# Queries and keys of an fp32 projection taken in two crosswise half-contractions on TensorE's two row groups, behind the last two score units of a turn

## The reference

```python
xn = layernorm(x)                                   # no scale, no shift
q, k, v = xn @ wq[h] + bq, xn @ wk[h] + bk, xn @ wv[h] + bv        # 16 heads of 8 columns
att = softmax(q k^T / sqrt(8)) v                    # per head, 256 x 256
a = concat(att) @ wo.T + bo
xr, xk = mu_r*xn + (1-mu_r)*prev(xn), mu_k*xn + (1-mu_k)*prev(xn)  # prev: one token back
f = sigmoid(xr @ W_r) * (square(relu(xk @ W_k)) @ W_v)
out = x + a + f
```

## Time and profile before

| | |
|---|---|
| median of 3 runs | 490.2 us (489.94 to 491.75) |
| the profiled execution's own time | 489.46 us |
| its span in the trace | 487.1 us |
| mean granted TensorE clock over the span | 0.971 |
| busy: TensorE, VectorE, ScalarE, GpSimd | 461.3, 422.2, 385.6, 339.6 us |

### The profile page before, as it was taken

How to read it: one execution, slowest core, us unless ns; L and a number is a source line. 1 busy time by engine, 2 the same in 40 slices (tenths; PEclk the granted TensorE clock), 3 DMA queues, 4 the chain that set the end, 5 groups by cost and what they waited for, 6 DMA issues and landing times.

```text
span 487.1 us, 15612 instructions
## 1 busy us (share of the span) xinstructions
PE 461.3 (95%) x5238; PEld 263.7 (54%) x5238; DVE 422.2 (87%) x886; ACT 385.6 (79%) x834; POOL 339.6 (70%) x611
## 2 busy tenths in 40 slices
PE   5599999999999999999999999999999999999994
PEld 4145555555555555555555555555655555555452
DVE  7578999999989999899998999999998999988831
ACT  2038888888878888888888888888888888888883
POOL 6567778777777877777777777777787777766220
PEclk9559999999999999999999999999999999999998
DMA  4443355444344544344455454344444443445100
GB/s 140 131 119 95 118 154 150 127 137 140 109 124 142 152 129 144 117 118 125 131 153 143 129 145 123 102 133 142 152 147 126 132 124 109 134 137 143 46 15 22
DMA packets 85837, 60.43 MB, mean 124 GB/s; under 512 B 6192, under 2 KB 73392, under 8 KB 85808
## 3 DMA queue, kind: packets, MB, share of 16 engines
q1 hardware_dynamic: 85808, 60.06, 42.2%
HBM read 29.89 MB, written 29.36 MB: 122 GB/s over the span
## 4 chain that ended last, share of the span: by engine, by line
PE 86%; DVE 6%; issue 4%; ACT 2%; DMA 1%; DVEq 0%; ACTq 0%; SPq 0%; POOL 0%; POOLq 0%
PE bank_exp L613 24%; PE bank_val L565 24%; PE bank_max L623 5%; PE misc_b L689 4%; PE misc_a L640 4%; PE misc_a L659 4%; DVE neg_max L496 4%; PE misc_c L585 3%; PE misc_a L697 3%; PE misc_b L650 3%; PE misc_a L708 2%; PE misc_b L589 2%; PE misc_c L573 1%; PE misc_c L667 1%; PE misc_b L672 1%
## 5 line engine op out<-in xcount | busy, mean ns | idle before, releaser
L496 DVE TENSOR_REDUCE neg_max<-bank_max 128x2 f32<-128x512 f32 x512 | 329.4, 686 | 35.2 <-PE bank_max L623 30.4
L406 ACT ACTIVATE probs<-bank_exp 128x512 f32<-128x512 f32 x512 | 279.0, 597 | 46.1 <-PE bank_exp L613 43.6
L613 PE MATMUL bank_exp<-ops 51*128 51x256 bf16 x1024 | 169.9, 271 | 7.5 <-DVE neg_max L496 2.4
L623 PE MATMUL bank_max<-ops 48*128 48x256 bf16 x1024 | 176.8, 279 | 0.0
L565 PE MATMUL bank_val<-probs,val 128*25 128x256 f32 x2048 | 138.4, 383 | 1.2 <-ACT probs L406 1.2
L613 PEld LDWEIGHTS bank_exp<-ops 51*128 51x128 bf16 x1024 | 65.5, 94 | 109.2 <-issue 88.2
L565 PEld LDWEIGHTS bank_val<-probs,val 128*25 128x25 f32 x2048 | 56.5, 103 | 41.1 <-issue 20.2
L623 PEld LDWEIGHTS bank_max<-ops 48*128 48x128 bf16 x1024 | 61.9, 95 | 1.2
L365 POOL TENSOR_TENSOR rstd<-var_eps,minus_half 128x2 f32<-128x2 f32 x32 | 22.9, 714 | 38.2 <-DVE var_eps L528 38.2
L321 POOL TENSOR_SCALAR xn<-x_in,moments,rstd 128x128 f32<-128x128 f32 x62 | 49.3, 801 | 0.0
L360 POOL TENSOR_TENSOR mixed_x<-mixed_x,xn_t 128x512 f32<-128x512 f32 x32 | 40.6, 1269 | 2.5
(11 more groups left out here) (67 smaller groups left out, 612.5 us busy)
## 6 DMA issues: line engine op xcount, KB each, us to landing
ops<-spill SPq DMA_DIRECT2D x128, 192.0 KB, 3.3
spill<-qk_h SPq DMA_DIRECT2D x64, 192.0 KB, 3.3
spill<-qk_m SPq DMA_DIRECT2D x64, 128.0 KB, 1.9
x_in<-x SPq DMA_DIRECT2D x32, 128.0 KB, 2.2
spill<-qk_l SPq DMA_DIRECT2D x32, 128.0 KB, 1.8
y_out<-y SPq DMA_DIRECT2D x32, 128.0 KB, 1.9
ops<-shift SPq DMA_DIRECT2D x128, 6.0 KB
w<-weights SPq DMA_DIRECT2D x1, 448.0 KB, 2.9
```

What stands on the lines that cost most here:

```text
L406: nc.scalar.activation(probs[g % 2][:, u % G, :, :], bank_exp[u % 2][:, :, :], ACT.Exp, scale=SCALE).then_inc(exp_done[u], 1)
L496: nc.vector.tensor_reduce(out=neg_max[hf][:, :, r, pr], in_=bank_max[v % 2][:, :, :], axis=AX_X, op=ALU.max, negate=True).then_inc(max_don ...
L613: exp_mm = nc.tensor.matmul(bank_exp[r][:, i, :], ops[p][rows, hf, 1, pr, i * P:(i + 1) * P], ops[p][rows, hf, 0, pr, :], start=True, stop ...
L623: max_mm = nc.tensor.matmul(bank_max[r][:, i, :], of[rows, max_hf, 0, max_pr, i * P:(i + 1) * P], of[rows, max_hf, 1, max_pr, :], start=Tr ...
```

## The change

The two full projections become four half-contractions. `project` is replaced by `project_half`, called twice. Without `swap` (behind unit 14) it multiplies the queries' lower 64 channels in the lower row group into `misc_c` and the keys' upper 64 channels in the upper row group into `misc_b`, both with start and without stop. With `swap` (behind unit 15) it multiplies the other halves, crosswise, and adds them to the same banks. The first step has all the waits that `project` had. The second waits for both halves of the first, on two new semaphores. The hidden layer still stands behind it at u = 15.

```diff
+        qk_half = [sem(f"{a}_half") for a in "qk"]
...
-            def project(c, n, live):
-                moving = xn_t[(c + 3) % TURN][:, 1:1 + S]
-                pe.wait_ge(xn_t_done, n(3))
-                after(pe, shift_done[0], n(1))
-                after(pe, qk_rest_done[0], n(2))
-                if not live(2):
-                    pe.wait_ge(weights_in, 16 * N_WEIGHT_DMAS)
-                nc.tensor.matmul(misc_c[:, 0:S], w[:, W_Q, :], moving, start=True,
-                                 stop=True).then_inc(qk_psum[0], 1)
-                after(pe, val_done, n(1))
-                after(pe, qk_rest_done[1], n(2))
-                nc.tensor.matmul(misc_b[:, 0:S], w[:, W_K, :], moving, start=True,
-                                 stop=True).then_inc(qk_psum[1], 1)
+            def project_half(c, n, live, swap):
+
+                moving = xn_t[(c + 3) % TURN]
+                lower, upper = slice(0, RG), slice(RG, P)
+                if not swap:
+                    pe.wait_ge(xn_t_done, n(3))
+                    after(pe, shift_done[0], n(1))
+                    after(pe, qk_rest_done[0], n(2))
+                    after(pe, val_done, n(1))
+                    after(pe, qk_rest_done[1], n(2))
+                    if not live(2):
+                        pe.wait_ge(weights_in, 16 * N_WEIGHT_DMAS)
+                else:
+
+                    pe.wait_ge(qk_half[0], n(3))
+                    pe.wait_ge(qk_half[1], n(3))
+                q_rows, k_rows = (upper, lower) if swap else (lower, upper)
+                q_mm = nc.tensor.matmul(misc_c[:, 0:S], w[q_rows, W_Q, :], moving[q_rows, 1:1 + S], start=not swap,
+                                        stop=swap)
+                k_mm = nc.tensor.matmul(misc_b[:, 0:S], w[k_rows, W_K, :], moving[k_rows, 1:1 + S], start=not swap,
+                                        stop=swap)
+                for a, mm in enumerate((q_mm, k_mm)):
+                    mm.then_inc(qk_psum[a] if swap else qk_half[a], 1)
...
                     if u == HALF and live(2) and not live(1):
-                        project(c, n, live)
+                        project_half(c, n, live, False)
+                    if u == HALF + 1 and live(2) and not live(1):
+                        project_half(c, n, live, True)
...
-                    if u == 15 and live(3) and (live(1) or not live(2)):
-                        project(c, n, live)
+                    if u >= 14 and live(3) and (live(1) or not live(2)):
+                        project_half(c, n, live, u == 15)
```

## The result

The changed kernel takes 497.78 us (median of 4 runs, 496.38 to 499.3) against 490.07 (4 runs, 488.0 to 491.75): ratio 1.016, 95% interval 1.0109 to 1.0211. On a second chip it took 495.91 against 489.79, ratio 1.0134 (1.0085 to 1.0183). The forecast was 492.4, with 497.5 as the upper end. So 6 to 8 us were lost where about 2 were forecast.

What follows compares the result with a forecast made beforehand. TensorE's own sequence was taken as the bound, VectorE and ScalarE close behind. +0.06 us a turn over 30 turns (+1.8) and +0.3 at the start gave +2.1 to 2.2: 490.2 + 2.2 = 492.4 us, range 487.0 to 497.5.

Steps and rivals of the forecast that it cites:

- the halves run side by side and overtake: In each projection step on TensorE, two halves share 0.43 us, the keys' first starting before the queries' second.
- the exposed first weights: Ahead of the hidden layer on TensorE: a first weight load of 0.11 us, which the queries had before.
- the 0.09: On TensorE before and after the hidden layer: 0.09 us lost at each change between row groups and 128 rows.
- the self-wait: Ahead of step 2, TensorE waits for step 1's completion: a new cost of 0.16 us a turn.
- step 2 starts at about 1.04, 0.16 after unit 15 has ended: Times from unit 14's start: step 1 done at 0.83, weight load at 0.94, weights 0.11, then step 2's stream.
- the bounds given: For the wait ahead of step 2: 0 to 0.30 us, the upper with two waits in series, each 0.07 more.
- the forecast case: The whole kernel at 490.5 to 494.5 us, with a chance of 0.52.
- A saving or a loss in one turn therefore counts about 30 times: Over the hidden layer's turns of 13.97 us: +0.06 us a turn, 30 turns, gives +1.8 us.
- ScalarE's stretch as unbroken: ScalarE shows no idle time from the queries to units 0 and 1's exponentials, so a 0.25 us delay passes on.
- slower through ScalarE: Rival: ScalarE's 0.25 us delay is not absorbed, +0.13 a turn on top, +6.0 in all, 496.2 us; chance 0.18.
- The start: At the first projection, two steps and the wait delay the first operands: +0.3 us once, bounds 0 and 0.75.
- a third of 0.52 with 0.18 and 0.10: Chances for slower: a third of the 490.5 to 494.5 case, ScalarE's delay 0.18, strict matmul order 0.10; stated 0.42.

Runs made afterwards that it cites:

- the two runs with nothing between: Kernel before with the keys' full product waiting for the queries': 501.66 us; changed kernel with both steps behind unit 15: 508.5 us.
- the covered wait: Changed kernel with step 1 moved behind unit 13 ahead of the values' product and step 2 behind unit 14: 504.79 us, ratio 1.0324.
- the start left as before: Changed kernel with the first two projections as two full products each, as in the kernel before: 495.52 us, ratio 1.0141.
- no-wait run: Changed kernel with the second step taking the same halves as the first, so it needs no wait: 492.46 us, ratio 1.005.

## Why the prediction was wrong

**Right.** No time is saved on the stream; the halves run side by side and overtake; step 1 needs no change of mode and its weights are preloaded; unit 15 comes 0.66 after unit 14 (0.67); the hidden layer takes over the exposed first weights; the 0.09 ahead of it and behind it stay. The sign, and that the self-wait is the part that costs.

**The term that was mis-sized: "step 2 starts at about 1.04, 0.16 after unit 15 has ended".** The streams of step 2 start at 1.09 and 1.12, 0.20 and 0.23 after it. The first load comes 0.16 after the modelled end of step 1, not 0.11, and why is open (0.12 in the two runs with nothing between). And the loads of the two groups are not side by side but 0.04 apart (305.27 and 305.31). That isn't the wait's doing: with both steps behind unit 15 they are 0.03 apart in step 1 too (298.14 and 298.17), where the weights aren't preloaded either. So a turn's stretch cost +0.15, not +0.06: 30 x 0.09 = 2.7 us, the larger part of the miss. The value sits within the bounds given (though the 0.07 in the upper one came from no row); the forecast case was drawn too narrowly around the nearest row.

**The step that failed: "A saving or a loss in one turn therefore counts about 30 times".** The mechanism of the restart was missing altogether. I took all turns to be like the one that I read. Every fourth one of the loop is not: five times the loop restarts (the expectations above say six), and there unit 15's lateness of 0.36, which in a regular turn VectorE and ScalarE absorb, passes through ScalarE's loop code, the queries, the wait of VectorE and VectorE's loop code, one behind another, to TensorE. It costs 0.36 each time, 0.21 more than a regular turn's 0.15: 5 x 0.21 = 1.1 us. The rows for it were in the trace of before: the mean of 13.97 us a turn that I worked out stood against 13.88 from unit 0 to unit 0 in the turn that I read, and I didn't ask what the rest was. (The mean is 13.95: my 433.0 ran from the first matmul of the first hidden layer to the second of the last.)

**ScalarE.** I forecast the queries taken at 1.68; they are taken 1.72 after unit 14. In regular turns the delay is absorbed: unit 1 to unit 2 grows by 0.03, and 0.03 comes back behind unit 2. But my reading of ScalarE's stretch as unbroken was wrong. Before, it took the keys and the hidden layer at 300.06 and 300.50, each 0.03 to 0.04 after the modelled end of its product, so TensorE paced it, with short idle times between. That is why the queries are 0.32 later and the exponential of unit 0 only 0.15 (2.71 after unit 14, where it was 300.82 - 298.26 = 2.56), no later than TensorE itself. The rival "slower through ScalarE" was right about the chain (the covered wait shows it) and wrong about where it bites. That its 496.2 us lie next to the measured 495.9 is luck: it had +0.19 in every turn and nothing more at the restarts.

**The start** was forecast at +0.3. The first operands are later, but the first hidden layer isn't, and with the start left as before the median didn't move beyond its scatter (495.52 and 495.91).

**The chances** don't quite follow from each other: a third of 0.52 with 0.18 and 0.10 makes 0.45 for slower, where I put 0.42.

Together 30 x 0.15 = 4.5, 1.1 for the restarts and 0.5 in the last two turns (looked into by no run) give 6.1 us, where 2.1 were forecast: 2.7 more from the mis-sized wait, 1.1 from the restarts, 0.5 from the last two turns, which I had put at nothing more, and 0.3 less at the start. The second chip measured 6.1. The first measured 7.7, with four runs a side, and its interval takes in 6.1.

## What to carry to other kernels

Read several turns of a loop, and always the one in which the loop restarts: divide the span by the number of turns, and if the mean is above the turn that you read, find the long one. In an engine's program, put the operation that waits for a late input behind the loop's end rather than ahead of it, so that the loop's own instructions run during the wait. A product split over row groups of one accumulator, with a wait of TensorE for itself between the parts as here, pays about 0.39 us from stream to stream (no run tried the right halves without the wait): split only if that much other work of TensorE stands between the parts, and count who waits for that other work.

## What the runs showed of the hardware

- fp32 half-contractions of 64 rows in the two row groups run fully side by side (0.43 us for two of 256 columns), and matmuls of different row groups start out of program order.
- A wait of TensorE for its own matmul costs 0.38 to 0.39 us from stream to stream: 0.16, 0.12 and 0.11 as above.
- The register and branch instructions of one restart of the loop left VectorE idle for 0.50 us behind its last operation, and ScalarE for 0.32 us ("issue" in the no-wait run).
- The same kernel's first turn took 15.31 us in one profile and 16.20 in another, with mean clocks of 0.63 and 0.50 from 36 to 42 us. When the high level is granted at the start varies between executions. A single profile should not be charged for it.
